# Identity products ahead of the attention, weights for the gates prepared later, and fewer late steps in the fourth layer's units

## The reference

```python
h = jnp.maximum(_layernorm(x, axis=-1), 0.0)
x = x + _L0_gnn_ref(h, adj, L0_gnn_W, L0_gnn_a)          # 4-head graph attention: masked softmax, att @ xp
h = jnp.maximum(_layernorm(x, axis=-1), 0.0)
x = x + _L1_gnn_ref(h, adj, L1_gnn_W_self, L1_gnn_W_neigh)  # h @ W_self + (adj @ h / deg) @ W_neigh
h = jnp.maximum(_layernorm(x, axis=-1), 0.0)
x = x + _L2_gnn_ref(h, adj, ...)                          # relu((adj @ h) @ W_msg.T + b), then a GRU cell
h = jnp.maximum(_layernorm(x, axis=-1), 0.0)
x = x + _L3_gnn_ref(h, adj, ...)                          # hyperbolic layer
```

```python
def log_map_zero(y):
    n = _norm(y)
    return jnp.arctanh(jnp.clip(n, 0.0, MAX_TANH)) * y / n
def exp_map_zero(v):
    n = _norm(v)
    return jnp.tanh(n) * v / n
neigh = exp_map_zero(adj @ log_map_zero(h))
out = exp_map_zero(log_map_zero(jnp.concatenate((x, neigh), axis=1)) @ layer)
out = h_add(out, layer_bias[None, :])   # needs the dot of every row with the bias
```

## Time and profile before

| | before |
|---|---|
| median of three runs | 593.09 us |
| the profiled execution's own time | 593.54 us |
| its span, first to last instruction | 591.7 us |
| TensorE products busy | 556.8 us, 94% |
| VectorE busy | 346.8 us, 59% |
| ScalarE busy | 217.2 us, 37% |
| GpSimd busy | 99.1 us, 17% |
| mean granted TensorE clock | 0.984 |

### The profile page before, as it was taken

One profiled execution on the slowest core, in us unless ns is written; L12 is line 12 of the kernel. 1 busy time (PEld: TensorE's weight loads), 2 busy tenths in 40 slices (PEclk: granted clock), 3 DMA queues, 4 the chain that ended last, 5 costly groups with the idle time before them and its releaser, 6 DMA issues.

```text
span 591.7 us, 12155 instructions
## 1 busy us (share of the span) xinstructions
PE 556.8 (94%) x4562; PEld 350.6 (59%) x4562; DVE 346.8 (59%) x1504; ACT 217.2 (37%) x588; POOL 99.1 (17%) x102
## 2 busy tenths in 40 slices
PE   4679899999999999999999999999999999999990
PEld 4579899999994544444444545555554444555540
DVE  5894822343224463333315588898888863676787
ACT  4530011100110200000032587888789665532433
POOL 3880000000000010000000121212222210330322
PEclk9979999999999999999999999999999999999996
DMA  8999999999950000000000001001100020111011
GB/s 235 108 108 108 109 109 108 108 109 108 109 55 4 1 19 1 1 0 1 14 5 19 13 24 37 16 29 30 36 1 20 18 90 1 37 54 37 18 37 36
DMA packets 23897, 29.17 MB, mean 49 GB/s; under 512 B 11296, under 2 KB 11936, under 8 KB 23840
## 3 DMA queue, kind: packets, MB, share of 16 engines
q0 software_dynamic: 8704, 16.78, 28.2%
q1 hardware_dynamic: 15136, 11.62, 6.5%
HBM read 72.43 MB, written 4.19 MB: 129 GB/s over the span
## 4 chain that ended last, share of the span: by engine, by line
PE 79%; DVE 15%; issue 2%; POOL 2%; ACT 1%; DMA 1%; SPq 0%; DVEq 0%; POOLq 0%
PE acc L1605 46%; PE acc L1413 10%; PE acc L1414 10%; PE acc L1443 4%; PE acc L1450 3%; PE acc L1501 2%; PE acc L1433 1%; POOL rs L1068 1%; DMA x<-x_rows 1%; PE acc L1537 1%; POOL region_st L1068 1%; DVE x L1048 1%; DVE region_op L999 1%; DVE x L1051 1%; DVE hs_a L384 1%
## 5 line engine op out<-in xcount | busy, mean ns | idle before, releaser
L1605 PE MATMUL acc<-adj,hs_a 128*128 128x512 fp8e4 x1024 | 227.8, 379 | 0.9 <-issue 0.9
L1605 PEld LDWEIGHTS acc<-adj,hs_a 128*128 128x128 f16 x1024 | 99.3, 98 | 114.0 <-issue 1.4
L1413 PE MATMUL acc<-region_op,adj 128*128 128x133 f16 x1024 | 127.6, 224 | 5.2 <-issue 3.6
L1414 PE MATMUL acc<-region_op,adj 128*128 128x132 f16 x1024 | 127.7, 223 | 0.0
L1605 PE MATMUL acc<-adj,region_op 128*128 128x512 fp8e4 x512 | 118.3, 379 | 0.0
L1413 PEld LDWEIGHTS acc<-region_op,adj 128*128 128x128 fp8e4 x1024 | 101.1, 99 | 7.0 <-issue 3.7
L1414 PEld LDWEIGHTS acc<-region_op,adj 128*128 128x128 fp8e4 x1024 | 101.0, 99 | 0.0
L1605 PEld LDWEIGHTS acc<-adj,region_op 128*128 128x128 f16 x512 | 49.3, 98 | 54.4
L1068 POOL TENSOR_TENSOR region_st<-region_st,small 128x4 f32<-128x4 f32 (+1 forms) x39 | 44.9, 1151 | 200.7 <-ACT w L1202 128.9
L1068 POOL TENSOR_TENSOR rs<-rs,small 128x4 f32 (+3 forms) x27 | 30.9, 1145 | 273.5 <-DVE rs L401 270.8
L1181 ACT ACTIVATE hs_a<-rowbuf 128x512 f32 (+1 forms) x8 | 5.0, 630 | 115.9 <-DVE rowbuf L407 115.9
(11 more groups left out here) (251 smaller groups left out, 689.4 us busy)
## 6 DMA issues: line engine op xcount, KB each, us to landing
adj<-adj_pieces POOLq DMA_DIRECT2D x32, 512.0 KB, 65.9
p_rows<-rowbuf SPq DMA_DIRECT2D x8, 256.0 KB, 2.1
region_op<-p_rows SPq DMA_DIRECT2D x8, 256.0 KB, 3.1
out_rows<-x SPq DMA_DIRECT2D x7, 256.0 KB, 2.1
x<-x_rows SPq DMA_DIRECT2D x3, 512.0 KB, 7.3
region_st<-matrices SPq DMA_DIRECT2D x1, 768.0 KB, 9.5
x<-x_rows SPq DMA_DIRECT2D x2, 256.0 KB, 4.2
hT<-region_op SPq DMA_TRANSPOSE x32, 2.4
```

Of the source, the lines that this page charges most:

```text
L1413: mm(dst[:, 0:HI], adj8[:, it, jt, :], op0[:, jt, 0:HI], start=(jt == 0), stop=False)
L1414: last = mm(dst[:, 0:LO], adj8[:, it, jt, :], op0[:, jt, HI:OPW], start=False, stop=(jt == NT - 1))
L1605: last = mm(dst, hs[:, jt, part, :], adj8[:, c * TG:(c + 1) * TG, jt, :], start=(k == 0), stop=(k == 2 * NT - 1))
```

## The change

1. `keep_busy(count)` multiplies the fp32 identity with itself and writes to a part of PSUM that nobody reads then: 14 products ahead of the small transpose (L1402), 26 behind the small product (L1404).
2. `prepare_weights` ends after the split of the first nine matrices and signals `w16_ready` there. What the gates need (message scale, gate weights, squares of the biases) is a function `prepare_gates`, run after `attend(1)`.
3. The last adjacency tile comes in two transfers of half the size, with a semaphore of its own for the second half. TensorE waits for it after the first 16 pairs of that tile.
4. `AHEAD_1` goes from 44 to 48, and the small steps in aggregation 1 go from 45, 50, 57 to 49, 54, 60.
5. In the hand-written order four products of SECOND go ahead of `update_back`, and `own_part` and `embed` of the last group come after 30 products of THIRD rather than 26.
6. In `layer3` the mask is multiplied into the series and into the factor of the logarithms before the dots. Behind the logarithms two linked steps less are left. The last two dots of a unit move behind the tanh's argument.

```diff
@@ attention, VectorE
                 me.link(v.reciprocal(w_scale, floors))
-                me.link(v.reciprocal(msg_scale, msg_unscale))
-                me.step(v.tensor_tensor(msg_bias, b_msg, msg_scale, ALU.mult))
-                me.link(v.tensor_tensor(msg_scale, msg_scale, floor[:, M_MSG:M_MSG + 1], ALU.mult))
...
-                me.step(copy(w_unscale, floors))
+                me.link(copy(w_unscale, floors))
+                v.memset(small[:, 51:52], 0.0).then_inc(S["w16_ready"], 1)
+
+            def prepare_gates(me):
+
+                me.link(v.reciprocal(msg_scale, msg_unscale))
...
             attend(1, None)
+            prepare_gates(me)
@@ layer3, VectorE
-                me.step(v.tensor_scalar(C3(MASK3), C3(CLIP3), SERIES_BELOW, None, ALU.is_lt))
+                me.link(v.tensor_scalar(C3(MASK3), C3(CLIP3), SERIES_BELOW, None, ALU.is_lt))
+                me.step(v.tensor_tensor(C3(SER3), C3(SER3), C3(MASK3), ALU.mult))
+                me.link(v.tensor_scalar(C3(MASK3), C3(MASK3), -0.5, 0.5, ALU.mult, ALU.add))
+                me.step(v.tensor_tensor(C3(SER3), C3(SER3), C3(KAP3), ALU.mult))
+                me.step(v.tensor_tensor(C3(MASK3), C3(MASK3), C3(KAP3), ALU.mult))
...
+                row_dots(0, cols - 2)
                 dve.wait_ge(S["ln3_out"], u + 1)
                 me.link(v.tensor_tensor(C3(AT3), C3(LNP3), C3(LNM3), ALU.subtract))
-                me.link(v.scalar_tensor_tensor(C3(SER3), C3(AT3), -0.5, C3(SER3), ALU.mult, ALU.add))
-                me.link(v.tensor_tensor(C3(SER3), C3(SER3), C3(MASK3), ALU.mult))
-                me.link(v.scalar_tensor_tensor(C3(AT3), C3(AT3), 0.5, C3(SER3), ALU.mult, ALU.add))
-                me.link(v.tensor_tensor(C3(KAP3), C3(AT3), C3(KAP3), ALU.mult))
+                me.link(v.tensor_tensor(C3(AT3), C3(AT3), C3(MASK3), ALU.mult))
+                me.link(v.tensor_tensor(C3(KAP3), C3(AT3), C3(SER3), ALU.add))
...
-                me.link(v.tensor_tensor(C3(R3), C3(R3), C3(KAP3), ALU.mult))
+                me.step(v.tensor_tensor(C3(R3), C3(R3), C3(KAP3), ALU.mult))
+                row_dots(cols - 2, cols)
+                me.settle()
                 dve.wait_ge(S["th3_out"], u + 1)
@@ fetch, GpSimd
-                pool.dma_start(dst, src).then_inc(adj_in[it], 16)
+                if it < NT - 1:
+                    pool.dma_start(dst, src).then_inc(adj_in[it], 16)
+                else:
+                    pool.dma_start(dst[:, 0:1, :], src[:, 0:1, :]).then_inc(adj_in[it], 16)
+                    pool.dma_start(dst[:, 1:2, :], src[:, 1:2, :]).then_inc(S["adj_last"], 16)
@@ TensorE
+            def keep_busy(count):
+
+                for _ in range(count):
+                    mm(bank[6][:, 0:D], ident[:], ident[:], start=True, stop=True)
+
+            keep_busy(KEEP_1)
...
+            keep_busy(KEEP_2)
             pe.wait_ge(S["wlo_ready"], 1)
...
-            AHEAD_1 = 44
-            both_zero = {45: own_transposes, 50: own_self, 57: neighbours}
+            AHEAD_1 = 48
+            both_zero = {49: own_transposes, 54: own_self, 60: neighbours}
...
-                attend(it, range(NT)).then_inc(S["acc_full"], 1)
+                if it < NT - 1:
+                    attend(it, range(NT)).then_inc(S["acc_full"], 1)
+                else:
+                    attend(it, range(PIECE_T))
+                    pe.wait_ge(S["adj_last"], 16)
+                    attend(it, range(PIECE_T, NT)).then_inc(S["acc_full"], 1)
...
             embed(FIRST - 2)
+            aggregate(SECOND, 8, 12)
             update_back(FIRST - 1)
-            aggregate(SECOND, 8, 40)
+            aggregate(SECOND, 12, 40)
...
-            aggregate(THIRD, 20, 26)
+            aggregate(THIRD, 20, 30)
             own_part(FIRST - 1)
             embed(FIRST - 1)
             aggregate(FIRST, 40, 48)
             aggregate(SECOND, 40, 48)
-            aggregate(THIRD, 26, 48)
+            aggregate(THIRD, 30, 48)
```

More of the change, by code:

```diff
@@ L41 @@
 EARLY = 3
+KEEP_1, KEEP_2 = 14, 26
 PIECES = ((0, 1), (1, 2), (2, 4), (4, 6), (6, 8))
@@ L241, in build_graph_stack @@
             "consts_set", "dve_step",
-            "ve_ready", "rs_ready", "wa_full", "xn0_ready", "tr0_full", "hT0_ready", "xp_full", "xp_read",
+            "ve_ready", "rs_ready", "wa_full", "adj_last", "xn0_ready", "tr0_full", "hT0_ready", "xp_full", "xp_read",
             "sq0_ready", "var0_ready", "rs0_ready", "pwa_ready", "ext_ready", "gen_step", "extT_full", "diag_ready", "extall_ready", "spread_ready", "spreadall_ready", "shift_ready", "w_ready", "whi_ready", "wlo_ready", "y_ready", "hi0_ready", "op0_ready",
@@ L601, in prepare_weights @@
                 me.step(v.tensor_scalar(w_unsplit, floors, 1.0 / SPLIT, None, ALU.mult))
-                me.step(copy(w_unscale, floors))
+                me.link(copy(w_unscale, floors))
+                v.memset(small[:, 51:52], 0.0).then_inc(S["w16_ready"], 1)
+            def prepare_gates(me):
+                me.link(v.reciprocal(msg_scale, msg_unscale))
+                me.step(v.tensor_tensor(msg_bias, b_msg, msg_scale, ALU.mult))
+                me.link(v.tensor_tensor(msg_scale, msg_scale, w_unscale[:, M_MSG:M_MSG + 1], ALU.mult))
                 me.step(v.tensor_scalar(ih_scale, w_scale[:, M_HR:M_HN + 1], msg_unscale, SPLIT, ALU.mult, ALU.mult))
@@ L614, in prepare_weights @@
                                                    op1=ALU.add, accum_out=y2))
-                v.memset(small[:, 51:52], 0.0).then_inc(S["w16_ready"], 1)
             attend(0, None)
@@ L718, in general_attention @@
                 dve.wait_ge(turn, TURN_END + 1)
-                prepare_weights(Steps(dve, S["gen_step"]))
+                steps = Steps(dve, S["gen_step"])
+                prepare_weights(steps)
+                prepare_gates(steps)
                 with dve.Fori(0, OWN_EARLY) as g:
@@ L1011, in layer3, with row_dots @@
                 me.step(v.scalar_tensor_tensor(C3(SER3), C3(SER3), 1.0, C3(CLIP3), ALU.add, ALU.mult))
-                me.step(v.tensor_scalar(C3(MASK3), C3(CLIP3), SERIES_BELOW, None, ALU.is_lt))
-                dve.wait_ge(S["v3_ready"], (g1 + 1) * TG)
-                for t in range(cols):
-                    me.step(v.tensor_tensor_reduce(out=tile(dve_junk, t % TG), in0=tile(v_rows, t), in1=b3l, scale=2.0,
-                                                   scalar=0.0, op0=ALU.mult, op1=ALU.add, accum_out=col(DOT3, t)))
-                    if t == TG - 1:
-                        me.settle()
+                me.link(v.tensor_scalar(C3(MASK3), C3(CLIP3), SERIES_BELOW, None, ALU.is_lt))
[3 more added lines that the diff above has]
+                me.step(v.tensor_tensor(C3(MASK3), C3(MASK3), C3(KAP3), ALU.mult))
+                dve.wait_ge(S["v3_ready"], (g1 + 1) * TG)
+                def row_dots(t0, t1):
+                    for t in range(t0, t1):
+                        me.step(v.tensor_tensor_reduce(out=tile(dve_junk, t % TG), in0=tile(v_rows, t), in1=b3l, scale=2.0,
+                                                       scalar=0.0, op0=ALU.mult, op1=ALU.add, accum_out=col(DOT3, t)))
+                        if t == TG - 1:
+                            me.settle()
+                row_dots(0, cols - 2)
                 dve.wait_ge(S["ln3_out"], u + 1)
                 me.link(v.tensor_tensor(C3(AT3), C3(LNP3), C3(LNM3), ALU.subtract))
-                me.link(v.scalar_tensor_tensor(C3(SER3), C3(AT3), -0.5, C3(SER3), ALU.mult, ALU.add))
-                me.link(v.tensor_tensor(C3(SER3), C3(SER3), C3(MASK3), ALU.mult))
-                me.link(v.scalar_tensor_tensor(C3(AT3), C3(AT3), 0.5, C3(SER3), ALU.mult, ALU.add))
-                me.link(v.tensor_tensor(C3(KAP3), C3(AT3), C3(KAP3), ALU.mult))
+                me.link(v.tensor_tensor(C3(AT3), C3(AT3), C3(MASK3), ALU.mult))
+                me.link(v.tensor_tensor(C3(KAP3), C3(AT3), C3(SER3), ALU.add))
                 dve.wait_ge(S["ne3_ready"], u + 1)
```

## The result

| | before | changed |
|---|---|---|
| median of 15 runs | 593.24 us | 594.83 us |
| ratio, 95% interval | | 1.0022 [1.0013, 1.0031] |
| profiled execution, own time | 593.54 us | 595.94 us |
| its span | 591.7 us | 594.1 us |
| from the start of the last projection to the end of the span | 566.97 us | 568.14 us |

The forecast was 592.3 us in a range of 590.9 to 593.9; the changed kernel is above it. All ratios here compare fast executions, and a single slow one, of 2065.84 us in the run before_241, is left out of its ratio.

What follows compares the result with a forecast made beforehand. TensorE, busy 556.8 of 591.7 us, was taken as the bound through its idle times, clock and tail. Terms -0.87 + 1.77 + 0 + 0.2 - 0.25 gave 0.85 us faster, 592.25 us beside the median; range 590.9 to 593.9.

Steps and rivals of the forecast that it cites:

- the flag's 0.89 us stay, four products later: At TensorE's flag wait, with `AHEAD_1` at 48: the wait stays the same; worth 0, bounds 0 and -0.3 us.
- Identity products, -0.87: Ahead of the attention: products delay its start 2.7 us, full clock gives 1.92 back; 0.87 us lost.
- Rival A: Ahead of the attention: identity products cost one record each; 1.85 us faster in all, 591.2 us; chance 0.16.
- rival B: Ahead of the attention: the clock falls despite the identity products; 8.4 us lost there, 599.8 us; chance 0.05.
- Gates, +1.77: At `attend(1)`: preparing the gates' weights afterwards removes TensorE's 1.61 us wait for `acc_read`; 1.77 us gained.
- The adjacency's air: At the last two row tiles: tiles land 1.6 us (last) and 1.9 us (one before) ahead of TensorE; no new wait.
- The split, 0: At the last adjacency tile: two transfers instead of one gain nothing, since air remains; worth 0.
- Order, +0.2: At the third layer's end: 0.2 us gained, not 0.9, with a new wait of about 0.7 us for the tangent.
- Units, -0.25: In the fourth layer: third, fourth and last units lose 0.16 + 0.05 + 0.05; 0.25 us lost, bounds -0.2 and +0.5.
- The prediction is wrong if the attention starts before 34.5 or after 37: Test at the attention's first product, forecast to start at 35.6 us in the changed kernel's trace.

Runs made afterwards that it cites:

- before_241: Kernel before with 92 never-executed products added in the untaken general path behind TensorE's flag branch; ratio 1.0084 to the kernel before.
- after_pad: Changed kernel with 40 never-executed products added in the untaken general path behind TensorE's flag branch; ratio 0.9991 to the kernel before.
- before_pad: Kernel before with 88 never-executed products added in the untaken general path behind TensorE's flag branch; ratio 1.0038.
- before_217: Kernel before with 80 never-executed products added in the untaken general path behind TensorE's flag branch; ratio 1.0025.
- 249: Kernel before with 96 never-executed products added in the untaken general path behind TensorE's flag branch; ratio 0.9998.
- gates: Kernel before with only `prepare_gates` moved behind `attend(1)`; ratio 0.9978.
- keep_short: Kernel before with 9 and 15 identity products, and unexecuted products that keep the branch target's place; ratio 0.9988.
- best: Changed kernel with 9 and 15 identity products, the old fourth-layer units, and unexecuted products restoring the branch target's place; ratio 0.9967 to the kernel before.
- best_one: Same as best, but with the last adjacency tile in one transfer; ratio 0.9977 to the kernel before.
- order alone: Kernel before with only the hand-written order of the third layer's end changed; ratio 0.9996.
- after_8: Changed kernel with 8 never-executed products added in the untaken general path behind TensorE's flag branch; ratio 0.9996 to the kernel before.
- keep: Kernel before with only the 14 and 26 identity products, plus 48 unexecuted products that hold the branch target's place; ratio 1.0020.

## Why the prediction was wrong, step by step

- **The flag, "the flag's 0.89 us stay, four products later": the step that failed.** The term `AHEAD_1` was put at 0 and measured 1.40 us lost. I took the wait for a thing of the branch alone and asked what *work* was moved past it. What counted was where the *code* behind it had moved: the identity products, 80 products and 80 weight loads, and 16 instructions from the rest of the change (eight of them by the larger `AHEAD_1`) pushed the target until 12 instructions were left in its block. A wait of 1.80 us appeared; from start to start it costs 1.97, and net of the shorter first wait 1.40. after_pad and before_pad show it in both directions, before_217, 241 and 249 where the block ends. Without it the change would have been about neutral: with it repaired the kernel stands at 0.9991 and 0.9996, and both intervals reach to 1. Of the 2.02 us between the forecast (0.85 faster) and the trace (1.17 slower) the flag is 1.40, the identity products 0.48, the units 0.12.
- **Identity products, -0.87: right mechanism, size 1.35.** Two records each, as the earlier trace rows said, and all of the clock's 1.92 came back (1.95). Off was the length: 11.47 us where my chain gave 10.87, in five small pieces; the largest are the 26, which take 5.91 rather than 5.72, and the answer to the small transpose, 1.12 rather than 0.92. My terms gave 0.78, and the step from there to 0.87 had no row behind it. Rival A (one record each) and rival B (the clock falls anyway) are both refuted by one row each.
- **Gates, +1.77: right, 1.79.** So was the reason: no wait for `acc_read`. The adjacency's air, which I gave as 1.6 and 1.9 us, bounded nothing in the changed kernel, since the products spent what the gates gained; in gates and keep_short it did, sooner than I had said.
- **The split, 0: right** in this kernel (no tile is waited for), and of use once TensorE is some two us ahead of before, as in best against best_one. In keep_short, 1.95 us ahead, the last tile in one transfer is waited for too.
- **Order, +0.2: right, 0.16** (order alone 0.19), with the new wait for the tangent at 0.55 us where I had 0.7. Too small for the times to tell.
- **Units, -0.25: right in kind, size 0.37.** The third unit costs 0.18 by making TensorE wait, for which I had 0.16. The other 0.19 are the last ones, for which I had 0.10.
- **"The prediction is wrong if the attention starts before 34.5 or after 37":** it started at 37.43, with 1.23 us of that from the execution's own start; without these it would have been 36.20, inside. An absolute time was a poor test; the distance from the last projection is what the change sets.

Without the flag my terms, as measured, give -1.35 + 1.79 + 0.16 - 0.37 = 0.23 us faster, 593.0 beside the median of before, 593.24: inside the range. after_pad and after_8 are 0.55 and 0.89 us faster in their own traces; the flag's own wait, 0.56 and 0.33 instead of 0.89, is nearly all of the rest.

What was left over is the flag's own wait. It was 0.68 to 1.14 us in the eight kernels whose branch stands where it does before (0.68, 0.81, 0.87, 0.89, 0.92, 1.03, 1.08, 1.14), and 0.30 to 0.56 in the eight with identity products ahead of it, which move the branch itself by 96 to 168 instructions. The DMA records of the sixteen traces tell what ends it. In all of them TensorE goes on 1.34 to 1.45 us after a 16 KB transfer on the queue "instruction" has ended. That transfer starts 1.74 to 1.91 us before TensorE falls idle where `AHEAD_1` is 44, and 2.13 to 2.18 where it is 48. It takes 1.16 to 1.71 us in the first eight kernels and 0.99 to 1.29 in the others. In keep it starts 1.90 ahead, as before, but takes 0.99 instead of 1.33, which is nearly the whole difference between 0.47 and 0.89. Why the transfer is shorter there stays open; the branch's place alone wasn't tried.

## What to carry to other kernels

- A change that adds or removes instructions moves all code behind it. Where the program takes a branch over a long body, look behind the branch for a second idle time that ends with "issue", and try some unexecuted instructions inside the body: here 16 and 80 of them were worth 1.5 and 1.8 us, more than most of what was tuned.
- Filler work that holds the clock must end before what it waits for is ready. Nine and fifteen products held the clock as fourteen and twenty-six did, and the attention started no later than without them.
- Compare two traces from the last instruction ahead of the change, not from the span's start; here the starts differed by up to 2.3 us.

## What the runs showed of the hardware that was not expected

- Behind a taken branch TensorE goes on to the end of the block that it landed in, and the next block's instructions come 3.0 to 3.3 us after its first instruction there. With 28, 12, 4 and -4 instructions left the loss by the ratio was 1.5, 2.3, 5.0 and -0.1 us; behind the branch alone the traces have 0.74, 1.97, 4.0 and none.
- At the branch, too, TensorE waits for a 16 KB transfer of instructions: in sixteen traces it goes on 1.34 to 1.45 us after that transfer's end.
- 2.36 us idle there (before_241) were followed, from about 1.2 us after TensorE was at work again, by 3.5 us at a granted 0.56; 1.79 us idle (before_pad) by no window below 1.00 up to 200 us.
- Identity products in fp32 hold the granted clock at 1.00, with gaps of 0.66 us (keep_short) and 0.85 us (changed kernel) between the blocks.
